# Five-layer graph network on one core: edge sums in four column groups, layer norm and layer 0's first two aggregation chunks in earlier strips

## The reference

```
h = maximum(layernorm(x), 0)              # x: 3125 nodes x 128
for l in range(5):
    agg_x = segment_sum(h[src], dst) + h            # 103125 edges, sorted by dst
    agg_e = segment_sum(edge_attr @ EW.T + EB, dst) + EB
    h = concat(agg_x, agg_e) @ W1.T + B1            # 256 -> 256
    h = relu(batchnorm over nodes(h)) @ W2.T + B2   # 256 -> 128
    if l < 4: h = relu(h)
out = x + h
```

## Time and profile before

| | us |
|---|---|
| median of 3 runs (lowest, highest) | 639.05 (638.67, 639.54) |
| the profiled execution's own time | 637.87 |
| its span | 636.1 |
| PE busy | 596.2 (94%) |
| DVE busy | 332.5 (52%) |
| ACT busy | 252.4 (40%) |
| POOL busy | 56.7 (9%) |
| mean granted clock of PE (share of full) | 0.989 |

### The profile page before, as it was taken

How to read it: one execution, slowest core, us unless ns; L and a number is a source line. 1 busy time by engine, 2 the same in 40 slices (tenths; PEclk the granted TensorE clock), 3 DMA queues, 4 the chain that set the end, 5 groups by cost and what they waited for, 6 DMA issues and landing times.

```text
span 636.1 us, 13067 instructions
## 1 busy us (share of the span) xinstructions
PE 596.2 (94%) x5565; PEld 369.2 (58%) x5565; DVE 332.5 (52%) x695; ACT 252.4 (40%) x552; POOL 56.7 (9%) x61
## 2 busy tenths in 40 slices
PE   6789798988999988999999999999999999999996
PEld 6677687755566644844446644448544458444456
DVE  6999999977899955721214521116411118101126
ACT  0378977766666724601114411116211117011123
POOL 5650114410000000000000000000000000000000
PEclk9799999998999999999999999999999999999998
DMA  5990000000000000000000100000100000100024
GB/s 146 321 302 7 3 5 28 7 5 4 6 5 1 6 4 3 24 10 1 1 1 2 33 1 1 1 1 2 34 1 1 1 1 2 33 2 1 1 72 132
DMA packets 13321, 19.23 MB, mean 30 GB/s; under 512 B 2263, under 2 KB 7397, under 8 KB 13251
## 3 DMA queue, kind: packets, MB, share of 16 engines
q1 hardware_dynamic: 12099, 16.00, 8.4%
q0 software_dynamic: 1152, 2.20, 1.5%
HBM read 16.26 MB, written 1.60 MB: 28 GB/s over the span
## 4 chain that ended last, share of the span: by engine, by line
PE 59%; DVE 2%; ACT 1%; issue 0%; POOLq 0%; DVEq 0%
PE bank L1397 41%; PE bank L1458 9%; PE bank L1433 7%; PE bank L1428 2%; DVE bn_stats L1603 1%; ACT h L1528 1%; DVE bn_small L1609 0%; PE bank L257 0%; ACT bn_small L1524 0%; PE bank L283 0%; DVE h L1654 0%; DVE bn_small L1614 0%; DVE bn_small L1616 0%; DVE bn_small L1617 0%; DVE bn_small L1615 0%
## 5 line engine op out<-in xcount | busy, mean ns | idle before, releaser
L1397 PE MATMUL bank<-adj,h_pieces 128*128 128x504 bf16 (+1 forms) x1372 | 263.5, 351 | 0.0
L1397 PEld LDWEIGHTS bank<-adj,h_pieces 128*128 128x128 f16 x1372 | 123.0, 97 | 141.4 <-issue 10.2
L1603 DVE BATCH_NORM_STATS2 bn_stats<-bank 128x6 f32<-128x504 f32 (+1 forms) x70 | 42.7, 626 | 221.2 <-PE bank L1433 220.7
L1002 ACT ACTIVATE adj<-bank 128x450 bf16<-128x450 f32 x175 | 95.0, 548 | 59.4 <-PE bank L860 53.8
L1509 ACT ACTIVATE h<-bank 128x504 f32<-128x504 f32 (+1 forms) x28 | 15.2, 543 | 226.6 <-PE bank L1397 226.6
L488 DVE TENSOR_TENSOR h<-iota_lo,h 128x1536 bf16<-128x1536 bf16 (+2 forms) x95 | 86.1, 907 | 11.6 <-PE bank L860 9.4
L494 PE MATMUL bank<-adj,h_pieces 128*128 128x450 bf16 x343 | 83.8, 356 | 1.1 <-POOL adj L625 1.1
L852 PE MATMUL bank<-h 128*128 128x75 bf16 x1064 | 68.5, 200 | 16.4 <-DVE h L488 15.1
L852 PEld LDWEIGHTS bank<-h 128*128 128x128 bf16 x1064 | 55.3, 99 | 46.7 <-DVE h L488 23.8
L883 PE MATMUL bank<-h,adj 128*17 128x40 f32 (+11 forms) x1752 | 74.7, 201 | 7.1 <-DVE h L669 4.9
L883 PEld LDWEIGHTS bank<-h,adj 128*17 128x17 f32 x1752 | 64.9, 100 | 12.4 <-DVE h L669 9.8
(11 more groups left out here) (162 smaller groups left out, 365.0 us busy)
## 6 DMA issues: line engine op xcount, KB each, us to landing
adj<-attr SPq DMA_DIRECT2D x1, 2524.5 KB
adj<-attr SPq DMA_DIRECT2D x1, 1963.5 KB, 14.7
weights<-wpack SPq DMA_DIRECT2D x5, 323.0 KB, 2.9
out<-h SPq DMA_DIRECT2D x6, 256.0 KB
adj<-attr SPq DMA_DIRECT2D x1, 1402.5 KB, 6.3
adj<-attr SPq DMA_DIRECT2D x2, 561.0 KB, 4.9
h<-mpack SPq DMA_DIRECT2D x5, 179.0 KB, 2.3
adj<-order SPq DMA_DIRECT2D x2, 202.0 KB, 2.6
```

The source lines that it names most:

```text
L1002: nc.scalar.activation(out_view(u), bank_view(n % CNT_BANKS), ACT.Copy).then_inc(s_ev, 1)
L1397: last = nc.tensor.matmul(agg_ps[b][:, 0:w], hp[:, k, s, :], adj[:, k, c * LW:c * LW + w], start=(k == 0 and s == 0), stop=stop and s == p ...
L1603: V.bn_stats(stats[:, h, ds(c * 6, 6)], w1_bank(c, h)).then_inc(st_done, 1)
```

## The change

It edits the strips alone. (1) Successive products of the edge sums write to four different groups of 32 output partitions of the bank (`GROUP_COLS`, `COL_GROUPS`). For this each chunk of the sums is opened by one 128x450 product that writes zeros, the products accumulate, ACT takes out 128 partitions in place of 17, and `stack` contracts over 128 rows. (2) In each of strips 0 to 48, PE gets two products of 384 columns whose result nobody reads. (3) Layer norm sums and squares go three tiles to a strip in place of two, and normalise two in place of one, from earlier strips (`SQUARES_AT` 20 to 16, `NORM_AT` 36 to 29); picks move from strip 32 to 24, overflow keys from 45 to 37, the first two overflow batches from 56 and 60 to 42 and 50. (4) Layer 0's chunks 0 and 1 run in strips 49 to 60 and 62 to 73, the other four in 78 to 100, 103 to 125, 128 to 150 and 153 to 174; chunks 0 and 1 are taken out in strips 76 and 77. (5) The transposed keys use one bank in place of two in turn, since the other takes the unread products. (6) The checks are spread over strips 74 to 98.

```diff
+GROUP_COLS = 32
+COL_GROUPS = P // GROUP_COLS
-WARM_START, WARM_TAIL = 45, 4
+WARM_START, WARM_TAIL, WARM_STEP = 45, 4, 2
-SUMS_AT, SQUARES_AT, SHIFT_AT, NORM_AT = 7, 20, 34, 36
+SUMS_AT, SQUARES_AT, SHIFT_AT, NORM_AT = 7, 16, 27, 29
-PICK_AT, OV_KEYS_AT, CHECK_AT = 32, 45, 74
+PICK_AT, OV_KEYS_AT, CHECK_AT = 24, 37, 74
+MOMENTS, NORMS = 3, 2
-OV_AT = (56, 60, 74, 98, 124, 148, 170)
+OV_AT = (42, 50, 74, 98, 124, 148, 170)
-AGG0_AT, AGG0_SPAN = 68, 106
+AGG0_STRIPS = ((49, 61), (62, 74), (78, 101), (103, 126), (128, 151), (153, STRIPS))
+AGG0_OUT = (76, 77)
...
 def agg0_steps(u):
-    n = CHUNKS * NODE_TILES - NODE_TILES
-    return [(j // NODE_TILES, j % NODE_TILES) for j in range(n) if AGG0_AT + j * AGG0_SPAN // n == u]
+    return [(c, k) for c, (a, b) in enumerate(AGG0_STRIPS) for k in range(NODE_TILES) if a + k * (b - a) // NODE_TILES == u]
...
                         pe.wait_ge(s_key, 2 * b + 2)
-                        if b >= 2:
-                            pe.wait_ge(s_kout, 2 * b - 2)
-                        bank = agg0_ps[b % 2]
+                        if b >= 1:
+                            pe.wait_ge(s_kout, 2 * b)
+                        bank = agg0_ps[0]
...
-                                opens = c not in begun
-                                if opens:
+                                g = (i * RUN + q) % COL_GROUPS
+                                if c not in begun:
                                     begun.add(c)
                                     if c >= 2:
                                         pe.wait_ge(s_sums, c - 1)
-                                last = nc.tensor.matmul(att_ps[c % 2][0:REC, a - c * CW:b - c * CW],
+                                    nc.tensor.matmul(att_ps[c % 2][:, 0:CW], ident, ident_pad[:, 0:1].to_broadcast([P, CW]),
+                                                     start=True, stop=True, skip_group_check=True)
+                                last = nc.tensor.matmul(att_ps[c % 2][g * GROUP_COLS:g * GROUP_COLS + REC, a - c * CW:b - c * CW],
                                                         attr_i[:, k, t * REC:(t + 1) * REC],
                                                         dst_oh[:, i % DST_SLOTS, q * DW + a - c0:q * DW + b - c0],
-                                                        start=opens, stop=True, skip_group_check=True)
+                                                        start=False, stop=True, skip_group_check=True)
...
+                        if u < AGG0_STRIPS[0][0]:
+                            for n in range(WARM_STEP):
+                                nc.tensor.matmul(agg0_ps[1][:, 0:3 * P], iota_lo[:, :], iota_lo[:, :].unsqueeze(1).to_broadcast([P, 3, P]),
+                                                 start=True, stop=True)
...
-                        if u == CHECK_AT + 4:
+                        if u == CHECK_AT + 16:
                             dve.wait_ge(s_chk0, 1)
                             dve.wait_ge(s_off, 4)
                             V.tensor_reduce(bad[:, 6:7], bad[:, 0:6], AX.X, ALU.add).then_inc(s_bad, 1)
```

More of the change, by code:

```diff
@@ L185, in half_at, with ln_tiles, high_unit, agg0_outs @@
     return HALVES.index((c, h))
-def ln_tiles(u, at):
-    return range(2 * (u - at), min(2 * (u - at) + 2, NODE_TILES)) if at <= u else ()
+def ln_tiles(u, at, n):
+    return range(n * (u - at), min(n * (u - at) + n, NODE_TILES)) if at <= u else ()
+def high_unit(u):
+    i, odd = divmod((u - NORM_AT - 2) * NORMS, 4)
+    return i if 0 <= i < UNITS and not odd else None
 def agg0_steps(u):
-    n = CHUNKS * NODE_TILES - NODE_TILES
-    return [(j // NODE_TILES, j % NODE_TILES) for j in range(n) if AGG0_AT + j * AGG0_SPAN // n == u]
+    return [(c, k) for c, (a, b) in enumerate(AGG0_STRIPS) for k in range(NODE_TILES) if a + k * (b - a) // NODE_TILES == u]
+def agg0_outs(u):
+    late = [c for c, at in enumerate(AGG0_OUT) if at == u]
+    return late + [c for c, k in agg0_steps(u - 1) if k == NODE_TILES - 1 and c >= len(AGG0_OUT)]
 def gin_program(nc, x, first, dst_lin, pair_lin, order, dst_win, src, dst, attr, consts, wpack, mpack, out, rest_dram, starts, picks):
+    assert min(AGG0_OUT) > step_strip(STEPS - 1) + 7
     assert COLS % CHUNKS == 0 and CW % SC == 0 and CHUNKS % 2 == 1 and UNITS % 2 == 1
@@ L347, in gin_program @@
             ab0, ub0 = a_oh[0][:, 0:8].bitcast(F32), a_oh[0][:, 8:12].bitcast(F32)
-            sums = agg0[0:REC, 0:CW]
+            sums = agg0[:, 0:CW]
             at = CW
@@ L645, in _ @@
                             overflow_pairs()
-                        if u >= NORM_AT + 4 and (u - NORM_AT) % 4 == 0 and (u - NORM_AT) // 4 < UNITS:
-                            low_piece((u - NORM_AT) // 4 - 1)
+                        if high_unit(u) is not None and high_unit(u) < UNITS - 1:
+                            low_piece(high_unit(u))
                         for c in range(CHUNKS):
@@ L1013, in _ @@
                                     act.wait_ge(s_stk, 3 * c - 2)
-                                nc.scalar.activation(sums, att_ps[c % 2][0:REC, 0:CW], ACT.Copy).then_inc(s_sums, 1)
+                                nc.scalar.activation(sums, att_ps[c % 2][:, 0:CW], ACT.Copy).then_inc(s_sums, 1)
                             if at == 3:
@@ L1039, in _ @@
                                                      accum_out=bad[:, 4 + h:5 + h]).then_inc(s_off, 1)
-                        for k in ln_tiles(u, SUMS_AT):
+                        for k in ln_tiles(u, SUMS_AT, MOMENTS):
                             if k == 0:
@@ L1047, in _ @@
                                 nc.scalar.activation(ln_minus, ln_sum, ACT.Copy, scale=-1.0 / D).then_inc(s_minus, 1)
-                        for k in ln_tiles(u, SQUARES_AT):
+                        for k in ln_tiles(u, SQUARES_AT, MOMENTS):
                             if k == 0:
@@ L1056, in _ @@
                                                      ).then_inc(s_sd, 1)
-                        k = u - NORM_AT
-                        if 0 <= k < NODE_TILES:
+                        if high_unit(u) is not None:
+                            high_piece(high_unit(u))
+                        for k in ln_tiles(u, NORM_AT, NORMS):
                             if k == 0:
@@ L1061, in _ @@
                             normalise(k)
-                        if k >= 4 and k % 4 == 0 and k // 4 <= UNITS:
-                            high_piece(k // 4 - 1)
-                        for c, k in agg0_steps(u - 1):
-                            if k == NODE_TILES - 1:
-                                chunk_out(c)
-                    for c, k in agg0_steps(STRIPS - 1):
-                        if k == NODE_TILES - 1:
+                        for c in agg0_outs(u):
                             chunk_out(c)
+                    for c in agg0_outs(STRIPS):
+                        chunk_out(c)
                     chunk_out(CHUNKS - 1)
@@ L1209, in _ @@
                             pe.wait_ge(s_gev, u + 1)
-                            stack(SC).then_inc(s_gstack, 1)
+                            stack_general(SC).then_inc(s_gstack, 1)
                             pe.wait_ge(s_gpc, 2 * u + 1)
@@ L1248, in _ @@
                             nc.scalar.activation(out_view(u), bank_view(0), ACT.Copy)
-                            nc.scalar.activation(sums[:, 0:SC], att_ps[0][0:REC, 0:SC], ACT.Copy).then_inc(s_gev, 1)
+                            nc.scalar.activation(sums[0:REC, 0:SC], att_ps[0][0:REC, 0:SC], ACT.Copy).then_inc(s_gev, 1)
                             act.wait_ge(s_gstack, 3 * u + 1)
@@ L1739 @@
         consts[rows, M_B] = -1.0 if m_piece >= 2 else 0.0
-        consts[0:REC, STACK + t * REC:STACK + (t + 1) * REC] = np.eye(REC)
+        for g in range(COL_GROUPS):
+            consts[g * GROUP_COLS:g * GROUP_COLS + REC, STACK + t * REC:STACK + (t + 1) * REC] = np.eye(REC)
     consts[:, EPSC] = EPS
```

18 lines of the change are left out of this document (11 added, 7 removed).

## The result

The changed kernel takes 643.07 us (median of 6 runs, 641.55 to 644.60) beside 638.48 for the one before (6 runs, 636.43 to 639.54): ratio 1.0074, 95% interval 1.0053 to 1.0094. It is slower by 4.6 us, where +4.9 was forecast. The number was right, but the terms of two stretches, B and D, were not, so the stretches are worth more than the sum.

A forecast was written before the change was run, and what follows sets the result against it. DVE was taken as the bound until strip 67, PE from strip 84, neither between. Terms 6.8 + 6.6 - 4.7 + 0.6 - 4.4 = +4.9 took the median from 639.05 to 644.0 us; range 635 to 652, likeliest case 640.4 to 648.

The forecast's parts named there:

- B: Strips 49 to 67: PE becomes the bound with the moved chunks, 36.1 us in place of 29.5, +6.6.
- D: Strips 84 on: PE's products fall to 2 a strip, DVE becomes the bound, 69.5 us in place of 73.9, -4.4.
- It is the nearest row, since groups take away the streaming, not the issuing: Edge sums: products start 0.025 us apart as narrow ones did, so the step falls from 0.79 to 0.55.
- The row of narrow products: Profile before, step where chunks meet: 38 mostly narrow products, starts 0.027 apart, 0.025 for the narrowest.
- The second rival: Full fourfold overlap in the edge sums: step falls to 0.20 us, total -3.9, 635.2 us; chance 0.20.
- A: Strips 0 to 48: DVE stays the bound and moved layer norm and overflow work costs +6.8, bounds +2 to +11.
- 3.4 for low pieces: Strips 0 to 48: four low pieces come in, each making one DVE destination one-hot wait, 4 x 0.85 = 3.4 us.
- 1.0 for ACT: Strips 16 to 24: ACT with three squares takes 1.9 a strip against DVE's 1.65, mostly swallowed, but key transposes wait.
- the larger part of 1.1: Strips 0 to 48: unread products cost PE 0.32 a strip against 0.24 saved; some 12 strips at +0.1.
- C: Strips 68 to 83: checks no longer wait and the old half clock vanishes, 16.0 us in place of 20.7, -4.7.
- a half chance of +1.3: Near strip 78: PE, without products in strips 74 to 77, may lose its clock for 3.4 us; counted +0.6.
- this wait is of latency and stays: Strips 84 on: at four overflow batches DVE still waits 0.83 us for PE's counts; 5.0 in all with one-hots and gap.

The follow-up runs named there:

- norm_early: groups_alone plus the changed kernel's layer norm, with picks, keys, overflow batches, chunks and checks in their old places; 643.31 us, ratio 1.0076.
- chunks_later: Changed kernel with layer 0's chunk 2 in strips 78 to 104 and chunks 3 to 5 starting at 107, 131 and 155; 644.07 us, ratio 1.0074.
- norm_two: Changed kernel with layer norm sums and squares two tiles a strip, squares from strip 20, normalise from 34, chunks 0 and 1 in 51 to 61, 63 to 73; 646.62 us.
- checks_alone: Kernel before with only the checks spread over strips 74 to 98; 636.25 us, ratio 0.9959.
- add_in_gap: Changed kernel with the fourth overflow batch at strip 100 in place of 98 and chunk 3 in strips 104 to 126; 641.06 us, ratio 1.0050.
- three_edits: Changed kernel with norm_two's edit, no unread products and chunks_later's edit together; 646.71 us, ratio 1.0108.
- groups_alone: Kernel before with only the four column groups (opening zeros, 128 partitions taken out, stack over 128 rows), no unread products; 637.86 us, ratio 0.9985.

## Why the prediction was right in its number, and where it was wrong

**B, +6.6 forecast, +0.7 measured.** The failed step is "It is the nearest row, since groups take away the streaming, not the issuing". Products start 0.010 us apart where I held 0.025 for the least; a step far under 0.5 us was the first sign of being wrong that the forecast named, and it came. The row of narrow products showed products of one and the same group of columns that follow each other, and so a bound of one group, not of the issue. The second rival, full fourfold overlap, had B at +0.7 and was right on it (its own terms, 18 x 1.41 + 1.2 + 2.6 + 0.7, make 29.9 and not 30.2; likewise its A, 6.8 less 1.1 and 1.3, comes to +4.4 and not +3.9). The rule of the Trainium skill that I had set against the row is TensorEngine Tiling (Array Packing), section Theoretical Speedup: up to 4 times. It held here, with products at 0.010 us in place of 0.036.

**A, +6.8 forecast, +5.3 to +8.0 in the profiles of the kernels that share it.** The size held, and the working only in part. I had 3.4 for low pieces that hold up destination one-hots, 0.85 each. The price was right and what they hit was not. Overflow keys on DVE, before and after:

```profile
94.13 0.47 DVE L695 TENSOR_SCALAR adj<-adj,picked_start_and_first 7x128 f32<-7x128 int32 x2
```

```profile
88.02 2.22 DVE L715 TENSOR_SCALAR adj<-adj,picked_start_and_first 7x128 f32<-7x128 int32 x2
```

With the instruction ahead of them (0.28 before, 1.21 after) and one strip one-hot, four instructions of DVE in A are some 0.9 us longer beside low pieces, 3.6 in all, where before two were, 1.5. The destination one-hots of A themselves got shorter (612 ns in the mean for 636). And I had 1.0 for ACT with the words that its excess is "mostly swallowed". norm_early speaks against it: in strips 16 to 28, where POOL does nothing, ACT has 2.3 us more to do and the strips take 2.7 longer. The unread products, forecast at the larger part of 1.1, cost 2 to 3. In the profile of the changed kernel DVE also stands 3.5 us behind two blocks of keys in strips 16 to 28, in waits for which the profile names no engine; chunks_later has none of this and A 2.7 shorter. How the cost of the layer norm divides between three squares a strip, two normalises a strip and the low pieces is not settled: norm_two and norm_early each brought a wait of their own.

**C, -4.7 and a half chance of +1.3 forecast, -3.3 measured.** The forecast counted -4.1. checks_alone gave -3.6 by the same mechanism. The half clock near strip 78 didn't come in the changed kernel's profile (clock 1.00), but did in six of the eight others with its chunks and checks. Without it C took 17.4 in all three profiles; with a spell of 3.4 us it took 17.9 to 18.4, with one of 6.8 us 19.1 and 19.2. So the chance was fair, and 0.5 to 1.1 is the price of a spell for which I had 1.3.

**D, -4.4 forecast, +0.1 measured.** The pace was right: -3.4 outside strips 100 to 103. The failed step is "this wait is of latency and stays", in the sense that I asked only what DVE loses in its gaps, and not who lives in them. A DVE that becomes the bound leaves POOL none, and +3.5 comes back in one wait and the half clock behind it. add_in_gap shows that it hangs on the place of POOL's add.

So the forecast was 5.9 us too high in B, and too low by 4.5 in D, 0.8 in C, 1.2 in A and 0.9 before strip 0, in this profile. That these cancelled to 1.5, and against the medians to 0.3, was luck. The second rival had the mechanism of B and missed the time by 8: it had D at -4.4 and A at +3.9.

## What to carry to other kernels

Work that is moved to an engine with room must also find room on the engines that feed it: here PE had it, after the groups (98 more products in B for 0.7 us), and ACT, which had to normalise the last tile in strip 41 in place of 60, did not; the kernel got faster by the two edits that moved nothing of that. A gap of an engine that is about to become the bound may be where another does its work: look for whose instructions end there before closing it. An edit that moves one engine's work can put it behind a wait of its own, as in norm_two and norm_early: read the new waits before crediting the time to the theory. And a clock at half costs nothing while the engine isn't waited for, and something where it is, as behind strip 103; products that only keep it up are to be tried against leaving them out.

## What the runs showed of the hardware

- fp32 products of 128 rows, 17 columns of weights and 40 of data, each in two instructions, start 0.036 us apart in one group of 32 columns and 0.010 when neighbours lie in four different groups; their loads 0.035 and 0.008. Put back in one group (one_group), B is 10.7 us longer.
- A POOL add of 128x75 bf16 took 0.3 to 1.2 us in most places, but 4.04 us, or 6.86 with the waiting chunk set later, where it began in an unbroken stretch of DVE's bf16 one-hots, and 3.64 us at one place in strips 49 to 67 of three_edits where DVE had no gap either.
- Low pieces on POOL (fp32 and fp16) lasted 1.1 to 6.1 us in all the kernels. DVE instructions beside the short ones were some 0.9 us longer: 1.21 for 0.28, 2.22 for 0.47 (two), and in norm_early 4.62 for 1.13 (two one-hots beside three low pieces).
- PE at 1.2 GHz for 82 of the first 150 us left groups_alone no slower than the kernel before. In C, which has 17.4 us without a spell at half clock, one of 3.4 us cost 0.5 to 1.1.
